# First layer's attention: inverse row sums reach the free axis by DMA through a row in memory, not by TensorE transposes and ScalarE copies

## The chip, the cores and the metric

The kernel runs on one core of a Trainium2 chip. The core has five engines with a queue of their own each: TensorE (PE, with its weight loads PEld), VectorE (DVE), ScalarE (ACT), GpSimd (POOL) and SyncE (SP), which here issues every DMA. Engines meet through semaphores only, and each works off its queue in order. The metric is device time in microseconds of one execution. Before the change it is 4202.77 us, the median of 3 runs (4202.66 to 4202.93).

## What is computed

The input is x of shape (8, 32, 32, 512) in float32. Two layers follow each other; the change touches the first alone, and of it this is what matters:

```python
x_flat = x.reshape(b, seq, c)                       # b = 8 images, seq = 1024 tokens, c = 512
x_norm = _group_norm(x, gn_scale, gn_bias).reshape(b, seq, c)
qkv = x_norm @ w_qkv + b_qkv
q, k, v = jnp.split(qkv, 3, axis=-1)                # then 8 heads of 64 channels
weight = jnp.einsum('bhld,bhsd->bhls', q * scale, k * scale)
weight = jax.nn.softmax(weight, axis=-1)
out = jnp.einsum('bhls,bhsd->bhld', weight, v)
out = out.transpose(0, 2, 1, 3).reshape(b, seq, c) @ w_out + b_out
return (x_flat + out).reshape(b, h, w, c)
```

The second layer (a layer norm, a deformable sampling, a second attention with 256 keys, an MLP) is the same in both kernels.

## The kernel before

`layer0` goes through the 8 images one after the other and through the 8 heads of an image in turn. For each engine a function writes out its whole queue for an image: `sync_image`, `tensor_image`, `scalar_image`, `vector_image`, `gpsimd_image`. The order of the work is therefore fixed by hand; nothing schedules it.

**Steps.** An image has U = 64 steps, 8 for a head, numbered `i_`. Step i computes the scores of 128 queries against all 1024 keys on TensorE (L446 and L447: high and low part of the keys, four products of 128x512). VectorE takes the row maxima (L624), ScalarE the exponentials with the row sums (L589). Two steps later TensorE transposes these probabilities (L461, eight 128x128 pieces), ScalarE copies them to SBUF as the high part `ph` (L582), VectorE makes the low part `pl` (L641).

**Blocks.** Two steps make a block b of 256 queries (32 blocks in an image, NB = 4 in a head). TensorE multiplies `ph` and `pl` of a block with the values in two halves, at steps 2b + 5 and 2b + 6 (L482, eight products of 128x256 each). High and low part of v stand side by side, so the result has two halves of 64 partitions which must be added: ScalarE copies one half (`fold_t`, L568), VectorE adds the other (`fold_s`, L632). At the end GpSimd multiplies by the inverse row sums and writes the block's attention into `qk` (L723).

**The inverse row sums.** VectorE makes them after every second step, at step 2b + 3 (L645), as `row_inv`, with a query on each partition. The multiplication needs a query in each column, the same value on all 64 partitions. Two TensorE transposes of the broadcast column (L477, at the head of the first half of the block's products) and a copy by ScalarE (`fold_r`, L572) bring them there. `fold_r` and `fold_s` have two buffers each.

**Staging of a head.** The scores of head H need its queries and keys split in high and low parts, doubled over the partitions. SyncE first brings them with four DMAs of 256 KB (L388, L389), once the scores of the first 8(H - 1) steps are done (L385), that is when head H - 1 is about to begin. GpSimd then splits them (`stage`): part 0 (L702, L704) after the multiplication of block 4H - 6, part 1 (L708, L711) after that of block 4H - 5, part 2 (L714) after that of block 4H - 4. This holds for heads 2 to 7, so six times in an image; heads 0 and 1 are staged ahead. TensorE's first score of head H waits for the end of part 2. A "head start" below is the start of that first product on L446.

**Queue of SyncE** in an image: the copies of heads 0 to 7; the next image's x (`xtok`, L394), once all copies have landed; x again for the residual (`tok`, L401); the stores of the result (L404).

## Time and profile before

| what | value |
|---|---|
| median of 3 runs | 4202.77 us |
| the profiled execution's own time | 4202.9 us |
| its span, first to last instruction | 4200.2 us |
| mean granted TensorE clock | 0.99 |
| attention of the first layer | 8 images, in the first 2320 us or so |
| busy share PE / DVE / ACT / POOL | 96% / 71% / 61% / 31% |
| TensorE instructions | 22762 |

The page's slices of the span show TensorE at nine tenths or more in nearly all of the first layer. Times in the rows further down are microseconds from the first instruction; "idle before" is how long an engine stood still before the piece of work, with what ended it. Matmuls overlap in the array, so the duration of one is not what it adds to the queue: the distance between two starts is.

### The profile page before, as it was taken

How to read it: one execution, taken by the hardware profiler on the slowest of the kernel's cores; microseconds unless marked ns; L12 is line 12 of the kernel's file. 1: busy time of each engine (PE TensorE's matmuls, PEld its weight loads, DVE VectorE, ACT ScalarE, POOL GpSimd, SP SyncE). 2: the span in 40 equal slices, each digit the busy share in tenths (PEclk: the TensorE clock that was granted, in tenths of full speed). 3: DMA queues.
4: the chain of work that ended last, by engine and by line, in shares of the span. 5: the costliest groups of instructions: out<-in, count | busy, mean ns of one | idle time of the engine just before them, and what ended most of it. 6: DMA issues, size and time to landing. Idle time of an engine off the chain costs nothing. (4 is left out here: it accounts for less than half of the span.)

```text
span 4200.2 us, 64531 instructions
## 1 busy us (share of the span) xinstructions
PE 4046.5 (96%) x22762; PEld 3386.1 (81%) x22762; DVE 2986.1 (71%) x5141; ACT 2582.9 (61%) x5617; POOL 1304.7 (31%) x1423
## 2 busy tenths in 40 slices
PE   8999999999999999999999899999999999999999
PEld 6888888888878888888888568777777777777777
DVE  3984975947849849669488367768696868686866
ACT  3874856837838658568387147564656565555646
POOL 1432433433324324324234004141323323141504
PEclk9999999999999999999999899999999999999999
DMA  2121220221212212212211303030302121212212
GB/s 83 41 69 43 49 83 21 61 61 39 58 46 51 67 44 63 61 31 51 61 41 50 115 21 86 18 99 21 92 29 71 51 61 61 61 61 53 69 39 62
DMA packets 113127, 235.53 MB, mean 56 GB/s; under 512 B 17260, under 2 KB 33704, under 8 KB 112808
## 3 DMA queue, kind: packets, MB, share of 16 engines
q1 hardware_dynamic: 112808, 231.41, 20.7%
q8 instruction: 184, 3.01, 0.3%
q14 instruction: 135, 1.11, 0.1%
HBM read 80.35 MB, written 33.55 MB: 27 GB/s over the span
## 5 line engine op out<-in xcount | busy, mean ns | idle before, releaser
L624 DVE TENSOR_REDUCE a_neg_max<-a_ps 128x1 f32<-128x1024 f32 x512 | 624.7, 1222 | 336.9 <-PE a_ps L447 336.9
L582 ACT ACTIVATE a_ph<-a_ps 128x512 fp32r<-128x512 f32 x1024 | 557.0, 593 | 171.2 <-PE a_ps L461 168.2
L641 DVE TENSOR_TENSOR a_pl<-a_ps,a_ph 128x512 fp32r<-128x512 f32 x1024 | 654.3, 679 | 8.9 <-ACT a_ph L582 5.7
L589 ACT ACTIVATE a_prob<-a_ps,a_neg_max 128x1024 f32<-128x1024 f32 x512 | 572.2, 1118 | 17.5 <-DVE a_neg_max L624 11.8
L723 POOL TENSOR_TENSOR a_qk<-a_fold_s,a_fold_r 64x256 f32<-64x256 f32 x256 | 191.3, 747 | 1228.4 <-DVE a_fold_s L632 1228.4
L461 PEld LDWEIGHTS a_ps<-a_ident,a_prob 128*128 128x128 f32 x4096 | 469.8, 140 | 112.6 <-issue 46.9
L461 PE MATMUL a_ps<-a_ident,a_prob 128*128 128x128 f32 x4096 | 540.7, 274 | 17.2 <-DVE a_pl L641 16.1
L1744 POOL TENSOR_SCALAR b_prob<-b_prob,b_row_inv 128x256 f32<-128x256 f32 x512 | 247.5, 483 | 994.4 <-DVE b_row_inv L1653 958.5
L482 PE MATMUL a_ps<-a_ph,a_v 128*128 128x256 f32 x2048 | 550.7, 302 | 0.0
L482 PE MATMUL a_ps<-a_pl,a_v 128*128 128x256 f32 x2048 | 509.1, 282 | 0.0
L446 PE MATMUL a_ps<-a_kh,a_qs 128*128 128x512 f32 x1024 | 408.3, 399 | 11.9 <-POOL a_kl L714 11.9
L447 PE MATMUL a_ps<-a_kl,a_qs 128*128 128x512 f32 x1024 | 404.7, 395 | 0.0
L482 PEld LDWEIGHTS a_ps<-a_pl,a_v 128*128 128x128 f32 x2048 | 389.3, 190 | 0.3
L482 PEld LDWEIGHTS a_ps<-a_ph,a_v 128*128 128x128 f32 x2048 | 386.4, 189 | 0.3
L1584 DVE SCALAR_TENSOR_TENSOR b_acc<-b_qpad,b_dww,b_acc 128x256 f32<-128x256 f32 x880 | 363.8, 479 | 4.9
L1250 PE MATMUL b_ps<-b_qpad,b_diag 128*128 128x256 f32 x1312 | 324.1, 408 | 0.0
L1429 ACT ACTIVATE b_diag<-b_ident,b_dww 128x128 f32<-128x128 f32 x656 | 250.6, 399 | 109.1 <-PE b_ps L1250 59.7
L1250 PEld LDWEIGHTS b_ps<-b_qpad,b_diag 128*128 128x128 f32 x1312 | 249.4, 190 | 72.8
L1506 ACT ACTIVATE b_prob<-b_ps,b_neg_max 128x256 f32<-128x256 f32 x512 | 236.4, 483 | 27.0 <-DVE b_neg_max L1658 26.6
L446 PEld LDWEIGHTS a_ps<-a_kh,a_qs 128*128 128x128 f32 x1024 | 193.7, 189 | 43.9 <-POOL a_kl L714 21.7
L447 PEld LDWEIGHTS a_ps<-a_kl,a_qs 128*128 128x128 f32 x1024 | 194.1, 190 | 25.0
L248 PE MATMUL a_ps<-a_xh,wqkv_hi 128*128 128x512 f32 x512 | 200.3, 391 | 4.3 <-DVE wqkv_lo L353 4.3
(250 smaller groups left out, 9058.4 us busy)
## 6 DMA issues: line engine op xcount, KB each, us to landing
a_qs<-a_qk SPq DMA_DIRECT2D x128, 256.0 KB, 3.7
a_kl<-a_qk SPq DMA_DIRECT2D x128, 256.0 KB, 4.4
a_xtok<-in_x SPq DMA_DIRECT2D x64, 256.0 KB, 4.4
b_xs<-x SPq DMA_DIRECT2D x64, 256.0 KB, 4.7
b_qs<-b_qh SPq DMA_DIRECT2D x64, 256.0 KB, 3.0
b_qs<-b_ql SPq DMA_DIRECT2D x64, 256.0 KB, 3.7
b_z<-x SPq DMA_DIRECT2D x64, 256.0 KB, 3.3
out<-b_ot SPq DMA_DIRECT2D x64, 256.0 KB, 2.0
```

Source lines behind the costliest of these rows:

```text
L446: pe.matmul(bank, q_, kh[:, j, n], start=True, stop=False)
L447: mm = pe.matmul(bank, q_, kl[:, j, n], start=False, stop=True)
L461: mm = pe.transpose(ps[:, 4 + n % 2, kk * P:(kk + 1) * P], prob[:, u % 2, kt * P:(kt + 1) * P], ident[:])
L482: mm = pe.matmul(ps[:, 6 + b % 2, 0:256], v[:, h, kt, :], q_[:, b % 2, kt, :], start=kt == 0 and e == 0, stop=kt == TT - 1 and e == 1)
L582: act.activation(ph[:, b % 2, 4 * g:4 * g + 4, (u % 2) * P:(u % 2 + 1) * P], ps[:, 4 + n % 2, :].rearrange("p (k q) -> p k q", k=4), ACT.C ...
L589: act.activation(prob[:, i_ % 2, :], ps[:, 2 * (i_ % 2):2 * (i_ % 2) + 2, :] .rearrange("p a b -> p (a b)"), ACT.Exp, bias=neg_max[:, i_:i ...
L624: dve.tensor_reduce(neg_max[:, i_:i_ + 1], ps[:, 2 * (i_ % 2):2 * (i_ % 2) + 2, :] .rearrange("p a b -> p (a b)"), AX, ALU.max, negate=Tru ...
L641: dve.tensor_tensor(pl[here], ps[:, 4 + n % 2, :].rearrange("p (k q) -> p k q", k=4), raw(ph[here]), ALU.subtract).then_inc(pl_ok, 1)
L1250: mm = pe.matmul(ps[:, c, 0:NS], diag[:, e % DIAGS, :], src, start=first, stop=last)
L1429: act.activation(diag[:, e % DIAGS, :], ident[:], ACT.Copy, scale=dww[:, c, n:n + 1])\
L1584: dve.scalar_tensor_tensor(dst, src, dww[:, c, n:n + 1], dst, ALU.mult, ALU.add)\
L1744: pool.tensor_scalar(prob[:, u % 2, t, :], prob[:, u % 2, t, :], row_inv[:, c:c + 1], 0.0, ALU.mult, ALU.add).then_inc(sc_ok, 1)
```

## The change

The two transposes (L477) and the copy into `fold_r` (L572) are gone. SyncE does the work instead: for each block, once `inv_ok` says that the inverses are there, it stores the two columns of `row_inv` (128 partitions, 8 bytes each) as a row of 256 values in memory, waits until this has landed, and loads that row back, broadcast to the 64 partitions that need it. The row then has the two steps' values alternating, so the multiplication reads `fold_r` with a step of two. `fold_cp` counts one copy in place of two, TensorE no longer waits for `inv_ok` and `fold_cp` in front of a block, and GpSimd waits for the load.

SyncE works in order, so these pairs of DMAs stand among the others. The copies of head H, which used to wait for nothing but the scores, now stand behind the pairs of blocks 0 to 4H - 5. The loads of the next image's x stand one behind each of the last eight pairs.

```diff
+            def inverses(b):
+
+                h = b // NB
+                sp.wait_ge(inv_ok, at(inv_ok, b + 1))
+                sp.dma_start(inv_row[b].rearrange("(p n) -> p n", n=2), row_inv[:, 2 * b:2 * b + 2]).then_inc(iv_st, 16)
+                sp.wait_ge(iv_st, at(iv_st, 16 * (b + 1)))
+                if b >= 2:
+                    sp.wait_ge(att_ok, at(att_ok, b - 1))
+                sp.dma_start(fold_r[own_half(h), b % 2, :], inv_row[b].partition_broadcast(HD))\
+                  .then_inc(iv_ld[b % 2], 16)
+
+            copies(0)
+            copies(1)
+            for b in range(U // 2):
+                if b % NB == 0 and b // NB + 1 in range(2, NH):
+                    copies(b // NB + 1)
+                if b == U // 2 - TT:
+                    for j in range(2):
+                        sp.wait_ge(s_ld[j], at(s_ld[j], 64 * (NH // 2)))
+                inverses(b)
+                if more and b >= U // 2 - TT:
+                    t = b - (U // 2 - TT)
                     sp.dma_start(xtok[:, t, :], x[r + 1, t * P:(t + 1) * P, :]).then_inc(x_ld[t], 16)
...
                 if part == 0:
-                    pe.wait_ge(inv_ok, at(inv_ok, b + 1))
...
-                        pe.wait_ge(fold_cp, at(fold_cp, 2 * b - 2))
-                    for n in range(2):
-                        u = 2 * b + n
-                        pe.transpose(ps[:, 6 + b % 2, 256 + n * P:256 + (n + 1) * P],
-                                     row_inv[:, u:u + 1].to_broadcast([P, P]), ident[:])
...
-                        .then_inc(fold_cp, 1)
-                    if b >= 2:
-                        act.wait_ge(att_ok, at(att_ok, b - 1))
-                    act.activation(fold_r[own_half(h), b % 2, :], ps[own_half(h), 6 + b % 2, 256:512], ACT.Copy)\
                         .then_inc(fold_cp, 1)
...
                 pool.wait_ge(fold_add, at(fold_add, b + 1))
-                pool.wait_ge(fold_cp, at(fold_cp, 2 * b + 2))
...
+                pool.wait_ge(iv_ld[b % 2], at(iv_ld[b % 2], 16 * (b // 2 + 1)))
...
+                                   fold_r[own_half(h), b % 2, :].rearrange("p (q n) -> p n q", n=2),
```

`copies(h)` holds the lines that stood in the loop over heads before, unchanged.

SyncE's queue from the start of an image, before: the copies of heads 0, 1, 2 and 3, four DMAs each.

```order
10 L388 DMA a_qs<-a_qk 64x1024 [waits a_qk_sb]
11 L389 DMA a_kl<-a_qk 64x1024
...
18 L388 DMA a_qs<-a_qk 64x1024 [waits a_score,a_qk_sb]
19 L389 DMA a_kl<-a_qk 64x1024
20 L388 DMA a_qs<-a_qk 64x1024
21 L389 DMA a_kl<-a_qk 64x1024
22 L388 DMA a_qs<-a_qk 64x1024 [waits a_score,a_qk_sb]
23 L389 DMA a_kl<-a_qk 64x1024
```

The same place after: `a_inv_row` is the row in memory; rows 24 and 25 are the pair of block 3, rows 26 to 29 the copies of head 2.

```order
22 L400 DMA a_inv_row<-a_row_inv 128x2 [waits a_inv_ok]
23 L404 DMA a_fold_r<-a_inv_row 64x256 [waits a_att_ok,a_iv_st]
24 L400 DMA a_inv_row<-a_row_inv 128x2 [waits a_inv_ok]
25 L404 DMA a_fold_r<-a_inv_row 64x256 [waits a_att_ok,a_iv_st]
26 L393 DMA a_qs<-a_qk 64x1024 [waits a_score,a_qk_sb]
27 L394 DMA a_kl<-a_qk 64x1024
28 L393 DMA a_qs<-a_qk 64x1024
29 L394 DMA a_kl<-a_qk 64x1024
30 L400 DMA a_inv_row<-a_row_inv 128x2 [waits a_inv_ok]
31 L404 DMA a_fold_r<-a_inv_row 64x256 [waits a_att_ok,a_iv_st]
```

What moved: the copies of a head have come to stand behind four pairs, each with a wait for a result of VectorE and a wait for its own store.

TensorE's queue at the first block's products, before (transposes of the probabilities, the two transposes of the inverses, the products):

```order
317 L461 MATMUL a_ps<-a_ident,a_prob 128x128 x8
318 L477 MATMUL a_ps<-a_ident,a_row_inv 128x128 x2
319 L482 MATMUL a_ps<-a_ph,a_v 128x256
320 L482 MATMUL a_ps<-a_pl,a_v 128x256
321 L482 MATMUL a_ps<-a_ph,a_v 128x256
```

And after, at the same place:

```order
317 L485 MATMUL a_ps<-a_ident,a_prob 128x128 x8
318 L500 MATMUL a_ps<-a_ph,a_v 128x256
319 L500 MATMUL a_ps<-a_pl,a_v 128x256
320 L500 MATMUL a_ps<-a_ph,a_v 128x256
```

What moved: nothing but the two transposes, which are gone; all else on TensorE keeps its order.

## Rows read from the trace of the kernel before

**Rows 1.** Groups by line: name, shapes, count | busy us, mean ns | idle before.

```profile
L477 PE MATMUL a_ps<-a_ident,a_row_inv 128*128 128x128 f32 x512 | 97.8, 273 | 0.6 <-DVE a_row_inv L645 0.6
```

**Rows 2.** Timeline of TensorE, two steps inside a head: start, us, line, work.

```profile
701.08 0.40 PE L446 MATMUL a_ps<-a_kh,a_qs 128*128 128x512 f32 x1
...
702.88 0.38 PE L477 MATMUL a_ps<-a_ident,a_row_inv 128*128 128x128 f32 x2
...
704.05 0.40 PE L446 MATMUL a_ps<-a_kh,a_qs 128*128 128x512 f32 x1
...
706.80 0.40 PE L446 MATMUL a_ps<-a_kh,a_qs 128*128 128x512 f32 x1
```

**Rows 3.** The same view around the starts of heads 1, 2, 3 and 7, third image.

```profile
689.62 0.40 PE L446 MATMUL a_ps<-a_kh,a_qs 128*128 128x512 f32 x1
...
712.41 0.28 PE L482 MATMUL a_ps<-a_pl,a_v 128*128 128x256 f32 x1
713.01 0.50 PE L446 MATMUL a_ps<-a_kh,a_qs 128*128 128x512 f32 x1 [0.32 <-POOL a_kl L714]
...
736.37 0.50 PE L446 MATMUL a_ps<-a_kh,a_qs 128*128 128x512 f32 x1 [0.18 <-POOL a_kl L714]
...
831.67 0.50 PE L446 MATMUL a_ps<-a_kh,a_qs 128*128 128x512 f32 x1 [0.18 <-POOL a_kl L714]
```

**Rows 4.** Timeline of SyncE and TensorE: the copies of head 3 after the last score.

```profile
710.47 0.39 PE L447 MATMUL a_ps<-a_kl,a_qs 128*128 128x512 f32 x1
...
710.94 0.46 SPq L388 DMA_DIRECT2D a_qs<-a_qk  x1
...
712.74 1.19 SPq L389 DMA_DIRECT2D a_kl<-a_qk  x1
```

**Rows 5.** DMA issues on L389: least, median and longest time to landing.

```profile
DMA to landing us min/median/max: 3.6/4.4/6.0
```

**Rows 6.** The same of the stores to memory on L404 (256 KB each).

```profile
DMA to landing us min/median/max: 2.0/2.0/4.1
```

**Rows 7.** Timeline of VectorE after the start of head 2.

```profile
714.24 1.23 DVE L624 TENSOR_REDUCE a_neg_max<-a_ps 128x1 f32<-128x1024 f32 x1 [0.85 <-PE a_ps L447]
715.50 0.43 DVE L632 TENSOR_TENSOR a_fold_s<-a_ps,a_fold_t 64x256 f32<-64x256 f32 x1
715.96 1.29 DVE L641 TENSOR_TENSOR a_pl<-a_ps,a_ph 128x512 fp32r<-128x512 f32 x2
717.22 1.22 DVE L624 TENSOR_REDUCE a_neg_max<-a_ps 128x1 f32<-128x1024 f32 x1
718.36 1.28 DVE L641 TENSOR_TENSOR a_pl<-a_ps,a_ph 128x512 fp32r<-128x512 f32 x2
719.55 0.15 DVE L645 RECIPROCAL a_row_inv<-a_row_sum 128x2 f32<-128x2 f32 x1
719.97 1.23 DVE L624 TENSOR_REDUCE a_neg_max<-a_ps 128x1 f32<-128x1024 f32 x1 [0.26 <-PE a_ps L447]
```

**Rows 8.** Timeline of GpSimd: end of head 2's staging, then the staging of head 3.

```profile
710.57 2.38 POOL L714 TENSOR_TENSOR a_kl<-a_kl,a_kh 128x1024 fp32r<-128x1024 f32 x1
...
722.62 1.05 POOL L702 TENSOR_SCALAR a_kh<-a_qs 128x1024 fp32r<-128x1024 f32 x1
723.75 2.40 POOL L704 TENSOR_TENSOR a_qs<-a_qs,a_kh 64x1024 fp32r<-64x1024 f32 x1
727.52 0.74 POOL L723 TENSOR_TENSOR a_qk<-a_fold_s,a_fold_r 64x256 f32<-64x256 f32 x1 [1.37 <-DVE a_fold_s L632]
...
733.11 0.74 POOL L723 TENSOR_TENSOR a_qk<-a_fold_s,a_fold_r 64x256 f32<-64x256 f32 x1 [2.60 <-DVE a_fold_s L632]
733.93 2.38 POOL L714 TENSOR_TENSOR a_kl<-a_kl,a_kh 128x1024 fp32r<-128x1024 f32 x1
```

**Rows 9.** Who waited for L714: engine and line, us in total, times.

```profile
  PE a_ps L446: 11.9, 48
```

**Rows 10.** Timeline of TensorE: first scores of images 4, 5 and 6, and a wait.

```profile
1238.89 0.39 PE L446 MATMUL a_ps<-a_kh,a_qs 128*128 128x512 f32 x1
...
1525.22 0.39 PE L446 MATMUL a_ps<-a_kh,a_qs 128*128 128x512 f32 x1
...
1748.87 0.73 PE L508 MATMUL a_ps<-wout_hi,a_a 128*128 128x512 f32 x1 [2.19 <-DVE a_tok_a L656]
...
1813.18 0.39 PE L446 MATMUL a_ps<-a_kh,a_qs 128*128 128x512 f32 x1
```

**Rows 11.** Stretches: length, busy us by engine, granted clock (PEclk), DMA share, GB/s.

```profile
15.10:25.10 10.00, 4.62 (x6) 2.07 (x7) 8.58 (x16) 6.55 (x6) 1.02 (x1) 0.50 0.42 161
...
1749.00:1752.40 3.40, 3.40 (x9) 2.63 (x10) 3.40 (x5) 1.43 (x2) 0.00 (x0) 0.50 0.28 108
886.00:892.00 6.00, 3.77 (x17) 2.82 (x16) 6.00 (x7) 3.18 (x3) 1.53 (x1) 1.00 0.12 44
```

**Rows 12.** Timeline of ScalarE at the last block of an image.

```profile
867.96 0.38 ACT L572 ACTIVATE a_fold_r<-a_ps 64x256 f32<-64x256 f32 x1
```

More of the change, by code:

```diff
@@ L84, in layer0 @@
     QSCALE = 1.0 / HD
+    inv_row = nc.dram_tensor("a_inv_row", [U // 2, 256], F32, kind="Internal").ap()
     with ExitStack() as ctx:
@@ L161, in layer0 @@
         av_ps, fold_cp, fold_add, att_ok = sem("av_ps"), sem("fold_cp"), sem("fold_add"), sem("att_ok")
+        iv_st, iv_ld = sem("iv_st"), [sem(f"iv_ld{i}") for i in range(2)]
         ah_ok, al_ok, out_ps, res_ok, out_ok = sem("ah_ok"), sem("al_ok"), sem("out_ps"), sem("res_ok"), sem("out_ok")
@@ L164, in layer0 @@
                    xn_ok, xh_ok, xl_ok, pr_ps, qk_sb, vh_ok, vl_ok, staged, score, max_ok, exp_ok, tr_ps, ph_ok,
-                   pl_ok, inv_ok, av_ps, fold_cp, fold_add, att_ok, ah_ok, al_ok, out_ps, res_ok, out_ok]
+                   pl_ok, inv_ok, av_ps, fold_cp, fold_add, att_ok, iv_st, *iv_ld, ah_ok, al_ok, out_ps, res_ok, out_ok]
         nums = [s.num for s in cleared]
@@ L366, in layer0 @@
         EACH.update({s_ld[0].num: 256, s_ld[1].num: 256, o_st.num: 16 * TT, pr_ps.num: len(groups), qk_sb.num: n_qk})
-        EACH.update({s.num: U for s in (score, max_ok, exp_ok, fold_cp)})
+        EACH.update({s.num: U for s in (score, max_ok, exp_ok)})
         EACH.update({s.num: 2 * U for s in (tr_ps, ph_ok, pl_ok)})
-        EACH.update({s.num: U // 2 for s in (inv_ok, av_ps, fold_add, att_ok)})
+        EACH.update({s.num: U // 2 for s in (inv_ok, av_ps, fold_cp, fold_add, att_ok)})
+        EACH.update({iv_st.num: 16 * (U // 2), iv_ld[0].num: 16 * (U // 4), iv_ld[1].num: 16 * (U // 4)})
         EACH.update({staged.num: STAGE * NH, ah_ok.num: len(SPLIT_AT), al_ok.num: len(SPLIT_AT)})
@@ L379, in sync_image, with copies @@
             more = r + 1 < n_images
-            for h in range(NH):
+            def copies(h):
                 p, j = h // 2, h % 2
@@ L389, in sync_image @@
                     sp.dma_start(raw(kl[rows_, j, :]), qk[own_half(h), CT + p, :]).then_inc(s_ld[j], 16)
-            if more:
-                for j in range(2):
-                    sp.wait_ge(s_ld[j], at(s_ld[j], 64 * (NH // 2)))
-                for t in range(TT):
+            def inverses(b):
[18 more added lines that the diff above has]
+                    t = b - (U // 2 - TT)
                     sp.dma_start(xtok[:, t, :], x[r + 1, t * P:(t + 1) * P, :]).then_inc(x_ld[t], 16)
@@ L494, in out_tile @@
                     pe.wait_ge(fold_add, at(fold_add, U // 2 + t - 3))
-                    pe.wait_ge(fold_cp, at(fold_cp, U + 2 * (t - 3)))
                 else:
@@ L628, in vector_image @@
                     h = b // NB
-                    dve.wait_ge(fold_cp, at(fold_cp, 2 * b + 2))
+                    dve.wait_ge(fold_cp, at(fold_cp, b + 1))
                     if b >= 2:
@@ L721, in gpsimd_image @@
                 pool.wait_ge(fold_add, at(fold_add, b + 1))
-                pool.wait_ge(fold_cp, at(fold_cp, 2 * b + 2))
-                pool.tensor_tensor(qk[own_half(h), h // 2, (b % NB) * 256:(b % NB + 1) * 256],
-                                   fold_s[own_half(h), b % 2, :], fold_r[own_half(h), b % 2, :],
+                pool.wait_ge(iv_ld[b % 2], at(iv_ld[b % 2], 16 * (b // 2 + 1)))
+                pool.tensor_tensor(qk[own_half(h), h // 2, (b % NB) * 256:(b % NB + 1) * 256]
+                                   .rearrange("p (n q) -> p n q", n=2),
+                                   fold_s[own_half(h), b % 2, :].rearrange("p (n q) -> p n q", n=2),
+                                   fold_r[own_half(h), b % 2, :].rearrange("p (q n) -> p n q", n=2),
                                    ALU.mult).then_inc(att_ok, 1)
```

## The prediction

> **What bounds the kernel now.** I read the groups by line first, then the timelines of one head. TensorE is busy for 96% of the span. Two steps inside a head show what that means [rows 2]: the first scores start at 701.08, 704.05 and 706.80. The interval that holds the two transposes of the inverses is 2.97 us, the one without is 2.75 us, and TensorE stands still in neither. So it is TensorE's queue that sets the pace inside a head. The second thing to see is at a head's start [rows 3]. The last product of head 1 starts at 712.41, the products before it are 0.12 apart, so head 2 could start at 712.53; it starts at 713.01, released by GpSimd's L714. In all 48 staged heads TensorE waits for that line [rows 9]. The wait is small, but it says that GpSimd's staging ends just as it is needed: **whatever makes the staging later makes the head later, one for one.** From head 1 to head 7 of an image it is 831.67 - 689.62 = 142.05 us, so 23.68 us for each of six heads. Of this, 0.48 is the wait and 4 x 0.22 = 0.88 the transposes; TensorE by itself would need about 22.1 to 22.3 us after the change.
>
> **What is removed.** The profile's groups by line put 97.8 us on the transposes [rows 1], but matmuls overlap; the distance of starts gives 2.97 - 2.75 = 0.22 us for a pair. Times 256 blocks that is 56 us, if TensorE stays the bound. ScalarE loses a copy of 0.38 us in each block. It has slack inside a head, and the copy lies on the path only at the last block of an image, where it stands between TensorE's last product and the attention's end [rows 12].
>
> **What is added, and where it stands.** A store of 128 x 8 bytes, a wait for its landing, a load of 64 x 1 KB, for each of 256 blocks. For the multiplication itself these are hidden: the inverses of a block are ready at step 2b + 3, its sum is folded at step 2b + 6, some 7 us later, and a store and a load come to about 2 + 2 us by the stores' landing [rows 6]. VectorE just keeps up: two steps are 719.55 + 0.15 - 714.24 = 5.46 us of work for it, with one fold and one reciprocal in them [rows 7], against 2 x 2.75 = 5.50 us of TensorE. The loads of the next image and of the residual come later by some microseconds, and lie behind other work of TensorE at an image's end.
>
> **What is moved is the point.** The copies of head H leave SyncE's queue behind the pair of block 4H - 5. Before, they leave 0.08 us after the last score of head H - 2 has ended, so ahead of the start of head H - 1 (710.47 + 0.39 = 710.86, first copy 710.94) [rows 4]. Now they wait for the reciprocal of step 8H - 7, which falls behind the start of head H - 1, then for a store. That makes a closed loop from one head start to the next:
>
> 1. Head start to the end of the reciprocal: 719.55 + 0.15 - 713.01 = 6.69 us [rows 3, 7]. VectorE is busy without a gap from 714.24 on, so TensorE's missing transposes don't shorten this.
> 2. Hand over to SyncE: 0.08 [rows 4].
> 3. The store to its landing: not in the trace. Nearest are the 256 KB stores to memory, 2.0 at least and in the median, 4.1 at most [rows 6]. The new one moves 1 KB, but in 128 pieces; I take 2.0, since the 256 KB stores are the only stores there are, and keep 4.1 as the other end. Below 2.0 nothing in these rows goes.
> 4. Hand over 0.08, and the load's issue 0.5, as one copy's (0.46 us, the next right behind) [rows 4].
> 5. The four copies: the last is issued 712.74 - 710.94 = 1.80 after the first and lands 4.4 (median of both places) to 6.0 later [rows 4, 5]; as the last of four it waits behind the others, so I take 5.2, the middle: 7.0.
> 6. Hand over 0.08.
> 7. GpSimd's chain from part 0 to the end of part 2, with the multiplications of blocks 4H - 5 and 4H - 4 between, which are ready by then: 733.93 + 2.38 - 722.62 = 13.69 as it stands, less the two waits of 1.37 and 2.60, plus 0.08 for each of two gaps: 9.88 [rows 8]. The multiplication now reads `fold_r` with a step of two; no row has that. Bounds are 0 and the operation's own 0.74 us, twice, and nothing below 0, as it works on as many values as before. I take 0, since 64x256 in 0.74 us is the pace of one value after the other in any case.
> 8. GpSimd's end to TensorE's first product: 713.01 - 712.95 = 0.06 (L714 of head 2 ends 710.57 + 2.38 = 712.95) [rows 3, 8].
>
> Sum: 6.69 + 0.08 + 2.0 + 0.58 + 7.0 + 0.08 + 9.88 + 0.06 = **26.37 us**, against 23.68 before and some 22.2 that TensorE needs. So TensorE stands still for about 4 us at each of the 48 starts, and the gain inside the heads is swallowed: what TensorE saves, it waits longer.
>
> **The clock.** TensorE's waits in the first layer so far are 2.2 us at most [rows 10]. After such a wait of 2.19 us in image 5 the granted clock was 0.50 for 3.4 us, the 1.2 GHz level, while after the like wait of image 2 it stayed at 1.00, the 2.4 GHz level; at the kernel's start, with waits of 4 us and more, it was 0.50 for 10 us [rows 11]. The half-clock stretch cost image 5 (1813.18 - 1525.22) - (1525.22 - 1238.89) = 1.63 us. Waits of 4 us at each head should bring it about most times. In the loop TensorE has a part only in term 1, through two steps' scores, so I price it at half of that cost, 0.8 us for a head, with bounds 0 and 1.6.
>
> The Trainium skill, "TensorE: Matmul & The Clock Gate", section "Why this matters for your kernels", asks to avoid gaps of some microseconds between bursts of matmuls, since the clock goes back to half after them. By the Trainium skill each head start here would come at the half clock; by the 2.2 us waits of this trace, one of which brought the half level and one of which did not, it could be none. The difference between the two is the 38 us of this term.
>
> **Sum.** (26.37 + 0.8 - 23.68) x 48 = 167.5 us. The first of the six loops in an image starts at a head that did not wait, 0.2 us less, x 8 = -1.6. Outside the six loops an image keeps about seven pairs of transposes, 7 x 0.22, and the last copy, 0.38: 1.9 x 8 = -15.2. Span 4200.2 + 150.7 = 4350.9; the execution's time is 2.7 us over its span (4202.9, which is the median within 0.2), so **4354 us**, 3.6% slower.
>
> **Rivals.**
> - *The clock holds* (no half level at head starts): 38 us less, 4316. For it speaks the 2.2 us wait of image 2, which left the clock alone; against it that 4 us is nearly twice that, and the start of the kernel. Chance 0.22.
> - *Small pieces are dear*: the store takes up to 4.1 us, or the strided multiplication up to 1.5 us more in the loop, or the four copies 6.0 instead of 5.2. Each microsecond in the loop is 48 us. With one of them at its end and the others where I have them: 4392 to 4455. Chance 0.18. The Trainium skill, "DMA: Bandwidth & Descriptors", section "Specifications", says that pieces under 512 bytes are done by read-modify-write, which would speak for a store over 2.0 us; no row of this trace has such a store.
> - *The staging keeps its cover*, and TensorE's 0.22 us a block is the gain: 4202.9 - 56 = 4147, and a bit less if the 0.5 us waits of the heads go too. The point at which it decides is a loop under 22.2 us: 4.2 us would have to be missing from my 26.37. That needs copies that land in 2.8 us instead of 7.0, or a queue of SyncE in which they don't wait for the store. The queue is plain to read, and every large term is a row. Chance 0.05.
> - *No difference*: the loop comes out near 23.4 us, 3 us under the sum, by copies that land faster and a quick store. Chance 0.02.
>
> **How the numbers follow.** Forecast 0.50 for 4330 to 4390, clock holds 0.22, dear pieces 0.18, cover 0.05, no difference 0.02, and 0.03 for a wait at the images' ends that I took as hidden. The likeliest gives 4354. The low end of the range takes in the steady clock with copies a bit under 7.0: 4285. The high end takes one dear piece nearly whole, 4450. Left out are the cases of no loss and both dear pieces together, less than 2 in 10. Faster 0.05, same 0.02, slower 0.93; 0.2% is about what a measurement of this kernel can tell from no change.
>
> **What would show it.** In the profile after, the distance of head starts should be about 27 us, with a wait of 3.5 to 4.5 us before L470 (the scores' first line there) released by GpSimd, 48 times, 170 to 200 us in total. GpSimd's first staging line (L702 before) should wait for the copies' DMA at heads 2 to 7, which it does at heads 0 alone now. Steps inside a head should be 2.75 us all. The new store's landing shows term 3, the multiplication's mean term 7, the granted clock in the first steps of a head the clock term. If the waits stand at another place, or the steps are not 2.75, the reading is wrong.

## The result, and the profile after

The kernel after takes 4533.62 us (median of 4 runs, 4527.79 to 4536.18) against 4202.72 us before in the same rounds: a ratio of 1.079, 95% interval 1.077 to 1.081. The forecast was 4354 with a range of 4285 to 4450. **The direction and the mechanism came as forecast, the size did not: the loss is 331 us, not 151.** The profiled execution took 4535.13 us with a span of 4533.4.

What the waits of the kernel after say (from the list of waits: who waited <- for whom: us in total, times, the longest):

```profile
POOL a_kh L715 <- DMA a_kl<-a_qk: 620.1, 56, 36.4
...
PE a_ps L470 <- POOL a_kl L727: 266.4, 48, 8.7
...
POOL a_qk L736 <- DMA a_fold_r<-a_inv_row: 182.2, 31, 44.6
```

L470 is the scores' first line (L446 before), L715 and L727 the first and last line of the staging (L702 and L714 before). Where 48 head starts waited 11.9 us in total [rows 9], they now wait 266.4; and GpSimd's staging now waits for the copies at 56 heads, all but the 8 heads 1. Both are the places that the prediction named. The last of these lines is one that it did not name: in 31 places a multiplication waits for its row. Of these, 22 are the last three blocks of an image, 29 to 31; in blocks 4 to 28, where the loops are, it is 7. The 44.6 us are an image's first block, which waited as long before (44.8 at most, for VectorE's fold).

One head start and the steps behind it on TensorE, third image (start, us, work; answers to [rows 2, 3]):

```profile
828.86 0.79 PE L470 MATMUL a_ps<-a_kh,a_qs 128*128 128x512 f32 x1 [5.52 <-POOL a_kl L727]
...
833.67 0.40 PE L470 MATMUL a_ps<-a_kh,a_qs 128*128 128x512 f32 x1
...
836.41 0.40 PE L470 MATMUL a_ps<-a_kh,a_qs 128*128 128x512 f32 x1
...
839.17 0.40 PE L470 MATMUL a_ps<-a_kh,a_qs 128*128 128x512 f32 x1
...
840.86 1.16 PE L485 MATMUL a_ps<-a_ident,a_prob 128*128 128x128 f32 x8 [0.60 <-DVE a_pl L654]
...
842.81 0.40 PE L470 MATMUL a_ps<-a_kh,a_qs 128*128 128x512 f32 x1
...
858.56 0.80 PE L470 MATMUL a_ps<-a_kh,a_qs 128*128 128x512 f32 x1 [4.45 <-POOL a_kl L727]
```

The steps that begin at 833.67 and 836.41 take 2.75 us, and the 2.97 of the steps with transposes is gone: their gain is there. But it is not whole. The step that begins at 839.17 takes 3.64 us, since TensorE waits 0.60 us for VectorE's `pl` in it. Heads 3, 5 and 7 have such a step (3.37 us before), heads 2, 4 and 6 have two of 2.88. The first step takes 4.81 us, and from this head's start to the next it is 29.70 us, where it was 23.68 on average before. The stretch behind the start (length, busy us of PE, PEld, DVE, ACT and POOL with counts, granted clock, DMA share, GB/s):

```profile
829.00:835.00 6.00, 6.00 (x28) 5.29 (x29) 3.07 (x5) 2.29 (x4) 0.73 (x1) 0.66 0.06 14
```

The same 6 us behind a head start before, right behind the one at 713.01 [rows 3]:

```profile
713.00:719.00 6.00, 5.99 (x43) 5.55 (x44) 5.09 (x9) 4.80 (x11) 0.74 (x1) 1.00 0.69 143
```

TensorE is busy all the time in both, but does 28 pieces of work in place of 43: granted clock 0.66, a mixture of the 1.2 and the 2.4 GHz level. By the trace's granted clock all 48 staged heads start at the half level. The half-clock stretch begins 0.5 to 5.1 us before the start, so inside the wait, and goes on for 2.9 to 6.1 us behind it, 4.8 in the mean. The page's slices, each some four heads long, show it only faintly, six of the first 25 at 8 tenths (one before):

```profile
PEclk9999899899999899899999898999999999999999
```

The other members of the loop in the same head. VectorE (answers to [rows 7]; the bracket is the idle time before):

```profile
830.97 1.23 DVE L637 TENSOR_REDUCE a_neg_max<-a_ps 128x1 f32<-128x1024 f32 x1 [5.17 <-PE a_ps L471]
...
834.79 1.23 DVE L637 TENSOR_REDUCE a_neg_max<-a_ps 128x1 f32<-128x1024 f32 x1 [0.80 <-PE a_ps L471]
...
837.13 0.15 DVE L658 RECIPROCAL a_row_inv<-a_row_sum 128x2 f32<-128x2 f32 x1
```

SyncE (answers to [rows 4]): the pair of the block, the four copies, the next pair.

```profile
837.31 0.33 SPq L400 DMA_DIRECT2D a_inv_row<-a_row_inv  x1
840.14 0.44 SPq L404 DMA_DIRECT2D a_fold_r<-a_inv_row  x1
840.68 0.54 SPq L393 DMA_DIRECT2D a_qs<-a_qk  x1
...
842.56 1.21 SPq L394 DMA_DIRECT2D a_kl<-a_qk  x1
...
849.92 0.46 SPq L404 DMA_DIRECT2D a_fold_r<-a_inv_row  x1
```

GpSimd (answers to [rows 8]):

```profile
848.66 1.06 POOL L715 TENSOR_SCALAR a_kh<-a_qs 128x1024 fp32r<-128x1024 f32 x1 [7.68 <-DMA a_kl<-a_qk]
...
852.28 0.73 POOL L736 TENSOR_TENSOR a_qk<-a_fold_s,a_fold_r 64x256 f32<-64x256 f32 x1
...
856.16 2.34 POOL L727 TENSOR_TENSOR a_kl<-a_kl,a_kh 128x1024 fp32r<-128x1024 f32 x1
```

Read as a chain: 828.86 start; 837.28 reciprocal done (8.42); 837.31 store leaves, 840.14 it has landed (2.83); 840.68 first copy, 848.66 the staging can begin (7.98); 858.50 it ends (9.84); 858.56 next head. Nothing in it is idle by choice, each link waits for the one before.

Landing times of the store (L400), then of the load (L404), least, median and longest of 256:

```profile
DMA to landing us min/median/max: 2.6/4.2/7.4
...
DMA to landing us min/median/max: 2.5/3.5/7.1
```

At the end of an image TensorE now waits where it did not (third image, the longest of seven, TensorE's first transpose of the next image's x; the others wait 1.9 to 4.2 us; before, this wait was 0.81 us):

```profile
995.17 1.09 PE L191 MATMUL a_ps<-a_ident,a_xtok 128*128 128x128 f32 x4 [5.01 <-ACT a_xt L195]
```

and GpSimd's last multiplication, one of the 31:

```profile
993.36 0.73 POOL L736 TENSOR_TENSOR a_qk<-a_fold_s,a_fold_r 64x256 f32<-64x256 f32 x1 [7.24 <-DMA a_fold_r<-a_inv_row]
```

### The profile page after: what moved, and what is told of

It reads as the page before. It is cut to its first block and busy times, and to the rows that moved or that the text cites. A ratio compares the mean times of both kernels' runs of the same rounds, so it can differ in the third digit from the quotient of the medians.

```text
span 4533.4 us, 63988 instructions
## 1 busy us (share of the span) xinstructions
PE 4111.8 (91%) x22250; PEld 3430.7 (76%) x22250; DVE 2994.5 (66%) x5141; ACT 2508.0 (55%) x5361; POOL 1306.1 (29%) x1423
## 5 line engine op out<-in xcount | busy, mean ns | idle before, releaser
L470 PE MATMUL a_ps<-a_kh,a_qs 128*128 128x512 f32 x1024 | 435.8, 426 | 266.4 <-POOL a_kl L727 266.4
L485 PE MATMUL a_ps<-a_ident,a_prob 128*128 128x128 f32 x4096 | 588.5, 289 | 21.7 <-DVE a_pl L654 20.6
L485 PEld LDWEIGHTS a_ps<-a_ident,a_prob 128*128 128x128 f32 x4096 | 502.4, 148 | 134.9 <-issue 72.3
L500 PE MATMUL a_ps<-a_ph,a_v 128*128 128x256 f32 x2048 | 576.9, 312 | 0.0
L500 PE MATMUL a_ps<-a_pl,a_v 128*128 128x256 f32 x2048 | 530.5, 290 | 0.0
L470 PEld LDWEIGHTS a_ps<-a_kh,a_qs 128*128 128x128 f32 x1024 | 208.4, 204 | 301.0 <-POOL a_kl L727 276.1
L471 PE MATMUL a_ps<-a_kl,a_qs 128*128 128x512 f32 x1024 | 427.5, 417 | 0.0
L500 PEld LDWEIGHTS a_ps<-a_pl,a_v 128*128 128x128 f32 x2048 | 409.0, 200 | 0.3
L500 PEld LDWEIGHTS a_ps<-a_ph,a_v 128*128 128x128 f32 x2048 | 408.0, 199 | 0.5 <-issue 0.2
L715 POOL TENSOR_SCALAR a_kh<-a_qs 128x1024 fp32r<-128x1024 f32 x64 | 67.4, 1053 | 620.8 <-DMA a_kl<-a_qk 620.1
L471 PEld LDWEIGHTS a_ps<-a_kl,a_qs 128*128 128x128 f32 x1024 | 209.5, 205 | 27.4
```

The source lines that it names most:

```text
L470: pe.matmul(bank, q_, kh[:, j, n], start=True, stop=False)
L471: mm = pe.matmul(bank, q_, kl[:, j, n], start=False, stop=True)
L485: mm = pe.transpose(ps[:, 4 + n % 2, kk * P:(kk + 1) * P], prob[:, u % 2, kt * P:(kt + 1) * P], ident[:])
L500: mm = pe.matmul(ps[:, 6 + b % 2, 0:256], v[:, h, kt, :], q_[:, b % 2, kt, :], start=kt == 0 and e == 0, stop=kt == TT - 1 and e == 1)
```

## The experiments

The theory is the prediction's closed loop: reciprocal, store, copies, staging, next head. Rivals are the clock, the small pieces and contention as the larger part. "Loop" below is the mean distance from one head start to the next over the 40 that end at heads 3 to 7 of the 8 images, where the loop is settled. The ratios are to the kernel before, timed beside each (4202.33, 4204.71, 4204.67 and 4202.63 us in the four groups of runs).

**e1_hoist: the copies ahead of the pairs again.**

```diff
-                if b % NB == 0 and b // NB + 1 in range(2, NH):
-                    copies(b // NB + 1)
+                if b % NB == 2 and b // NB + 2 in range(2, NH):
+                    copies(b // NB + 2)
```

> The changed kernel with one thing moved in SyncE's queue: the four copies of head H stand ahead of the pair of block 4H - 6, not behind the pair of block 4H - 5, so they leave when the scores of head H - 2 are done, as in the kernel before. Theory (the loss is the closed loop reciprocal, store, copies, staging): TensorE's waits at the 48 head starts fall from 266 us in total to under 20 us, a head takes about 22.3 us, and the time is 4202.9 - 56 plus the some 4 us by which each image's end got longer (gap before the transposes of the next image, 5.0 against 0.8 us), x 8: about 4180 us. Rival (the pairs of DMAs are themselves what costs: small pieces land after 4.2 us, the rows come after 3.5 us, and GpSimd's multiplications wait for them wherever the copies stand): heads stay above 26 us and the time above 4350.

Measured: 4337.44 us, ratio 1.033 (1.031 to 1.035), 196 us less than after. So the place of the copies is the larger part of the loss, but the 4180 us of the theory were missed by 157: the settled heads are 25.7 to 26.3 us apart, not 22.3. The rest is a new wait in the other direction: the row of block 4H - 6 now stands behind copies that wait for a score, and comes late. The multiplications of blocks 2, 6, 10, 14, 18 and 22 wait 6.4 to 11.4 us for it. The list of waits:

```profile
POOL a_qk L736 <- DMA a_fold_r<-a_inv_row: 764.9, 160, 44.6
...
PE a_ps L470 <- POOL a_kl L727: 119.8, 48, 5.9
```

The rival, that the pairs cost this wherever the copies stand, is answered by e10_inter below: the same pairs in memory, with heads of 23.1 to 24.0 us.

**e2_late: the kernel before with nothing but late copies.** The transposes stay, there are no pairs; the copies of a head wait for four scores more.

```diff
-                    sp.wait_ge(score, at(score, TT * (h - 1)))
+                    sp.wait_ge(score, at(score, TT * (h - 1) + 4))
```

> The kernel before, with its transposes and ScalarE copies, no pair of DMAs, and one thing changed: SyncE holds the copies of head H back until four more score steps are done (so until some 10 us after the start of head H - 1 at the full clock, 12 at the half one, where the changed kernel sends them at 12.2). Theory of the closed loop: the lateness alone makes the loss. Loop 12 + 7.0 + 0.1 + 9.9 = 29 us with the clock at half after the starts, 27 us if it holds, against 23.7: 4202.9 + 48 x 3.3 to 5.3 = 4360 to 4460 us, waits on GpSimd at 48 heads of 4 to 5 us each. Rival (traffic and latency of the new DMAs make the loss): hidden or nearly so, under 4250.

Measured: 4451.89 us, ratio 1.059 (1.058 to 1.061). Three quarters of the loss of the change, without one of its DMAs. TensorE's waits for the staging:

```profile
PE a_ps L446 <- POOL a_kl L714: 166.9, 48, 4.6
```

The first copy leaves 11.85 us behind the head start on average (12.30 in after), and the loop is 28.73 us. Lateness alone makes the loop; its clock came with it (mean 0.964, before 0.99).

**e3_busy: TensorE kept busy through the wait.** At each staged head start, 40 products of 128x256 whose result is overwritten come ahead of the wait for the staging, and behind the one for the exponentials; only work is added.

```diff
+                if t == 0:
+                    if h >= 2:
+                        for _ in range(40):
+                            pe.matmul(ps[:, 2 * (i_ % 2), 0:256], woh[:, 0, 0:P], woh[:, 1, 0:256], start=True,
+                                      stop=True)
+                    pe.wait_ge(staged, at(staged, STAGE * (h + 1)))
```

> The changed kernel with 40 products of 128x256 more on TensorE at each staged head's start, written to a bank that the head's first scores then overwrite, so that TensorE works where it stood still (some 4.8 us of work in a wait of 5.6). Theory (half clock after the wait costs 2.1 us of the loop, in the stretch from head start to the reciprocal: 8.8 us in place of 6.7): the granted clock stays at 1.0, that stretch is 6.7 us, the loop 28 us in place of 30.1, and the time falls by 48 x 2.1 = 100 us to about 4430, though TensorE has 230 us more to do. Rival (the clock is a symptom, the stretch is long for other reasons): the time stays at 4534 or rises.

Measured: 4463.83 us, ratio 1.0625 (1.061 to 1.064): 1920 useless products made the kernel 70 us faster. The stretch behind a head start (columns as above):

```profile
812.60:818.60 6.00, 6.00 (x42) 5.51 (x43) 4.79 (x7) 3.79 (x7) 0.75 (x1) 1.00 0.14 11
```

The granted clock is 1.00 in place of 0.66, 42 pieces in place of 28. From head start to the end of the reciprocal it is 6.75 us on average (after: 8.70), as expected. The loop is 28.92 (after: 30.55), so 1.63 us of the 1.95 arrive; the store and GpSimd's chain take 0.3 us longer here. That is the larger part of why 70 us came and not the 100 of the expectation.

**e4_wide: whole rows of 512 bytes in place of 8-byte pieces.** The store is made from `ident`, so values other than the inverses are loaded.

```diff
+    inv_row = nc.dram_tensor("a_inv_row", [U // 2, P * P], F32, kind="Internal").ap()
...
+                sp.dma_start(inv_row[b].rearrange("(p n) -> p n", n=P), ident[:]).then_inc(iv_st, 16)
...
+                sp.dma_start(fold_r[own_half(h), b % 2, :], inv_row[b, 0:256].partition_broadcast(HD))\
```

> The changed kernel with the store of each pair taken from the identity matrix, 128 pieces of 512 bytes in place of 128 pieces of 8; the row that is loaded back is part of that, so the attention is multiplied by other values than its inverse row sums. Theory (the store's 2.9 us when alone, where 256 KB stores take 2.0, is due to pieces of 8 bytes): it lands after 2.0 to 2.1 us, the loop is 0.8 us shorter, and the time falls by 40 us to about 4495. Rival (it is the price of a store next to the others, or of its 128 pieces whatever their size): within 10 us of 4534, or above it.

Measured: 4378.52 us, ratio 1.0415 (1.040 to 1.043): 155 us less than after, four times the 40 that I expected. Moving 64 times the bytes, the store lands sooner, and the load behind it too. L400, then L404:

```profile
DMA to landing us min/median/max: 1.5/1.5/5.1
...
DMA to landing us min/median/max: 2.4/2.5/3.5
```

This was the surprise, and the next kernels ask what about the pieces is slow.

**e7_pitch and e11_pitch64: the same 8-byte pieces, laid apart.** 512 bytes and 64 bytes from one to the next; the load reads 1 KB of mostly other values, and the rows in memory are filled once at the start.

```diff
+                sp.dma_start(inv_row[b].rearrange("(p n) -> p n", n=P)[:, 0:2], row_inv[:, 2 * b:2 * b + 2])
```

```diff
+                sp.dma_start(inv_row[b, 0:16 * P].rearrange("(p n) -> p n", n=16)[:, 0:2], row_inv[:, 2 * b:2 * b + 2])
```

> The changed kernel with the 128 pieces of 8 bytes stored 512 bytes apart in memory, each into a line of its own; the row that is loaded back is the first 1 KB there, so most of the attention is multiplied by other values than its inverses, and 32 stores at the start of the first image set the rest of the memory. Theory (a piece of 8 bytes is dear by itself): the store lands after 2.8 us or more as before. Rival (dear is that many pieces share a line of memory and are done one after the other): it lands after 1.5 to 1.6 us as the pieces of 512 bytes do, and the loop falls to 27.3 us.

> As e7_pitch, with the 8-byte pieces 64 bytes apart in place of 512, so eight of them in 512 bytes; most of the attention is multiplied by other values than its inverses. If the crowding is within 64 bytes, the store lands after 1.4 us as in e7_pitch; if within 512 bytes, between 1.4 and 2.9 us.

**e8_p256: pieces of 256 bytes side by side**, again from `ident`.

```diff
+                sp.dma_start(inv_row[b, 0:64 * P].rearrange("(p n) -> p n", n=64), ident[:, 0:64]).then_inc(iv_st, 16)
```

> As e4_wide, the store from the identity matrix and other values than the inverses, but with pieces of 256 bytes: two pieces share what one of 512 fills. If pieces under 512 bytes pay a read-modify-write each, it lands after 2.8 us as the 8-byte ones. If only the crowding of many pieces in a line costs, it lands at 1.5 to 1.8 us.

Measured: e7_pitch 4361.75 us, ratio 1.037 (1.035 to 1.039); e11_pitch64 4361.15, 1.037 (1.036 to 1.039); e8_p256 4364.57, 1.038 (1.036 to 1.040). All three agree with e4_wide within 18 us. The store of e11_pitch64 (L401), then of e8_p256 (L400):

```profile
DMA to landing us min/median/max: 1.4/1.4/4.7
```

```profile
DMA to landing us min/median/max: 1.4/1.4/4.8
```

So the number of pieces is not it, nor their size: 128 pieces of 8 bytes land in 1.4 us when each has 64 bytes to itself, and in 2.6 at the least when they are packed side by side. Pitches between 8 and 64 bytes were not run. The loads are 2.5 us in all three. Since these kernels load other memory than was written in small pieces, or only some of it, they don't tell whether the load of after is slower because its row was packed or because it was just then written; that stays open.

**e5_sbrow: the row in SBUF instead of in memory**, on one partition.

```diff
+        inv_row = R.take("a_inv_row", [1, 2, 256])
...
+                sp.dma_start(inv_row[:, b % 2, :].rearrange("o (p n) -> o p n", n=2), row_inv[:, 2 * b:2 * b + 2])
...
+                sp.dma_start(fold_r[own_half(h), b % 2, :], inv_row[:, b % 2, :].unsqueeze(1).to_broadcast([1, HD, 256]))\
```

> The changed kernel with the row of inverses kept in SBUF (one partition, two buffers) in place of memory: the same 128 pieces of 8 bytes, the same queue order, and the wait for the multiplication two blocks back ahead of the store. Theory (8-byte pieces are dear only when they are written to memory): the store lands after 2.0 us or less, the load after 2.0 to 2.5, the loop is 27.3 us as with the 512-byte pieces, and the time is 4350 to 4390 us. Rival (128 pieces of 8 bytes are dear wherever they go): the store lands after 2.8 us or more and the time stays at 4500 or above.

Measured: 4501.26 us, ratio 1.070 (1.068 to 1.072), 32 us less than after. Its store (L402), then its load (L404):

```profile
DMA to landing us min/median/max: 1.9/1.9/5.2
...
DMA to landing us min/median/max: 3.8/4.0/4.4
```

The theory missed by more than 110 us: its store came, its load did not. The time is the rival's, but not by the rival's slow store. In the loop the store gives 1.0 us (2.99 to 1.98), but the load lands later (4.0 for 3.5 us in the median), and the four copies behind it take 8.43 us from first issue to last landing (after: 7.94). **Here half of what the quicker store won went to slower copies behind a slower load.**

**e6_sbhoist, e9_sbinter and e10_inter: the copies moved back, with less in their way.** e6 is e5 with e1's edit. e9 is e5 with the copies between the store and the wait for it; e10 is the same with the row in memory.

```diff
+                if b % NB == 2 and b // NB + 2 in range(2, NH):
+                    copies(b // NB + 2)
                 sp.wait_ge(iv_st, at(iv_st, 16 * (b + 1)))
```

> e5_sbrow with the copies of head H two blocks earlier in SyncE's queue, as in e1_hoist. Theory (two causes and no third: copies behind the pairs, and slow pairs): both gone, the heads are bound by TensorE at 22.2 to 22.6 us, no half clock at their starts, and the time is 4150 to 4185 us, faster than the kernel before. Rival (SyncE's one queue is too busy in any case, store, wait, load and copies of 3 us in turn, so that GpSimd's multiplications still wait for a row): heads of 24 us or more, 4230 or above.

> The row of inverses in SBUF, and the copies of head H issued between the store and the load of block 4H - 6, so that SyncE issues them while that store is on its way (in e6_sbhoist they stood ahead of that store, the pair came 3 to 5 us late and the staging's first part waited for its multiplication). Theory: the multiplication of block 4H - 6 waits 1 to 2 us less for its row, the staging ends before the head is due, the waits at head starts fall under 0.2 us, a head takes 22.4 us in the mean, and the time is about 4130 us (4115 to 4150). Rival: the load now queues behind 1 MB of copies and lands no sooner, so heads stay at 23.4 us and the time at 4175 to 4190.

> The changed kernel, row in memory, with the copies of head H between the store and the load of block 4H - 6. Same theory: against e1_hoist (4337) the copies no longer hold back a pair, heads come down from 26.2 to 24 to 25 us, 4230 to 4290, still above the kernel before since store (4.2 to 4.7 us) and load (3.5 to 3.7 us) of every block fill SyncE's 5.5 us. Rival: if the slow stores were slow through the copies running beside them, heads at 22.5 us and 4150.

Measured: e6_sbhoist 4180.78 us, ratio 0.995 (0.993 to 0.996); e9_sbinter 4180.58, 0.994 (0.993 to 0.996); e10_inter 4206.77, 1.000 (0.9995 to 1.001). So one place in SyncE's queue turns a loss of 331 us into nothing (e10), and with the row in SBUF into a small gain. The expectations fared worse than that sounds. e6's time lies in its range, but its heads take 23.1 to 23.9 us and not 22.2 to 22.6, so the number was right by another way. e9 was expected at 4130 and came at its rival's 4175 to 4190: issuing the copies behind the store, not ahead of it, gave nothing over e6. e10 came below its 4230 to 4290. The settled heads of e9 and e10 are nearly alike inside an image (23.1 and 23.9 to 24.0 us by turns); what parts them is the image's end, 119 to 121 us from head 7 to the next image's first score in e9, 122 to 128 in e10. There the last multiplication waits for its row in all 8 images, 5.3 to 7.6 us, and the wait before L191 is 3.1 to 8.5 us (e9: under 0.8).

But 56 us were to be had from the transposes and 24 came. GpSimd before a head start of e9_sbinter shows one reason:

```profile
795.07 0.74 POOL L736 TENSOR_TENSOR a_qk<-a_fold_s,a_fold_r 64x256 f32<-64x256 f32 x1 [0.42 <-DMA a_fold_r<-a_inv_row]
...
797.02 1.05 POOL L724 TENSOR_SCALAR a_kh<-a_kl 128x1024 fp32r<-128x1024 f32 x1
800.25 0.76 POOL L736 TENSOR_TENSOR a_qk<-a_fold_s,a_fold_r 64x256 f32<-64x256 f32 x1 [2.17 <-DVE a_fold_s L645]
801.09 2.37 POOL L727 TENSOR_TENSOR a_kl<-a_kl,a_kh 128x1024 fp32r<-128x1024 f32 x1
```

Part 2 of the staging (L727) stands behind the multiplication of block 4H - 4, which waits 2.17 us for VectorE's fold. TensorE's next head starts at 803.51, right behind it. The staging hangs on a fold late in the head.

**e12_sbparts and e13_bparts: part 2 right behind part 1**, ahead of that multiplication; e12 on e9, e13 on the kernel before.

```diff
-                if 1 <= k <= NH - 2 and part < 3:
-                    stage(k + 1, (part,))
+                if 1 <= k <= NH - 2 and part < 2:
+                    stage(k + 1, ((0,), (1, 2))[part])
```

> e9_sbinter with part 2 of a head's staging moved from behind the multiplication of block 4H - 4 to behind part 1, so behind block 4H - 5. In e9_sbinter and e10_inter heads take 23.07 and 23.89 us in turn, though TensorE needs some 22.1, and L727 ends just before each start. Theory: what is left of the removed transposes' gain is eaten by that one wait, since part 2 hangs on the fold of step 8H - 2 and not on TensorE's queue. Then heads fall to 22.1 and 23.0 us, waits at the 48 starts vanish, and the time falls by 48 x 0.9 = 43 us to about 4138. Rival (VectorE, with 5.46 us of work for each 5.50 us, is the floor): heads come down by 0.3 us or less, 4165 to 4180.

> The kernel before, transposes and all, with only that move of part 2. By the theory above its heads lose only the waits of 0.5 and 0.2 us at their starts, 48 x 0.35 = 17 us, to about 4186, and the difference to e12_sbparts (48 us expected) is what taking the transposes off TensorE is worth once nothing else binds; 56 us was my figure for it. Rival (VectorE is the floor): both end at the same time.

Measured: **e12_sbparts 4155.27 us, ratio 0.989 (0.987 to 0.990), the fastest of all, below both kernels**; I had put it at 4138. e13_bparts 4197.20, 0.9985 (0.998 to 0.999), expected at 4186. In its heads the expected 17 us came (the six loops of an image fell from 142.05 to 139.96 us). But six of its seven image ends hold a half-clock stretch of 3.4 us, which the kernel before has in one, and they take 122.6 us in the mean for 121.1. GpSimd of e12:

```profile
786.72 1.05 POOL L724 TENSOR_SCALAR a_kh<-a_kl 128x1024 fp32r<-128x1024 f32 x1
787.85 2.40 POOL L727 TENSOR_TENSOR a_kl<-a_kl,a_kh 128x1024 fp32r<-128x1024 f32 x1
790.32 0.74 POOL L736 TENSOR_TENSOR a_qk<-a_fold_s,a_fold_r 64x256 f32<-64x256 f32 x1
```

L727 ends at 790.25, the next head starts at 792.94, and in the list of waits no row of TensorE behind L727 is left. The difference of e13 and e12 is 4197.20 - 4155.27 = 42 us, where 56 was the forecast of what the transposes are worth. It is not all theirs. By the spans (43.7 us) the six loops make 23 of it, the way from head 0 to head 1 makes 3, and the images' ends 18; some 6 of these are the half-clock stretch, which e12 has at two images' ends and e13 at six. Inside the six loops 42 us were forecast (24 pairs, 8 images, 0.22 us), so about half of it came. The other half did not come: some steps take 2.88 us for 2.75, with waits too short for the list, and some 3.6, where TensorE waits for the next in line, VectorE. List of waits of e12_sbparts (16.1 us in 48 places before, 25.0 in 72 in e13):

```profile
PE a_ps L485 <- DVE a_pl L654: 33.4, 72, 0.6
```

VectorE has 5.46 us of work in two steps, TensorE now 5.50. In heads 3, 5 and 7 VectorE has an operation more, twice: a low part of the attention (L662), with a wait for ScalarE in front of it. In the head of after shown above it stands ahead of TensorE's wait at 840.86:

```profile
837.97 0.69 DVE L662 TENSOR_TENSOR a_a<-a_qk,a_a 128x512 fp32r<-128x512 f32 x1 [0.68 <-ACT a_a L610]
```

In e12 TensorE waits 0.5 to 0.6 us for `pl` behind each of the two, these steps take 3.64 and 3.58 us, and the settled heads come 22.4 and 23.9 us apart by turns. The rival of e12, VectorE as the floor, had the time wrong but this part of the mechanism right.

**e14_xearly: the next image's x loaded ahead of the last eight pairs**, all eight at once, to see whether the wait at the image's end is for them.

```diff
+                    if more:
+                        for t in range(TT):
+                            sp.dma_start(xtok[:, t, :], x[r + 1, t * P:(t + 1) * P, :]).then_inc(x_ld[t], 16)
```

> The changed kernel with the eight loads of the next image's x issued together ahead of the pair of block 24, as in the kernel before, and not one behind each of the last eight pairs. Theory A (each image's end is 4 us longer because the last block's row comes late, behind those loads in the queues): the wait before the transposes of x at an image's end falls from 5.0 to about 1 us, and the time falls by 25 to 30 us to some 4505. Theory B (the row is late by its own slow store and load): the wait stays at 4 to 5 us and the time within 10 us of 4534, or rises as block 24 now waits behind 2 MB.

Measured: 4582.08 us, ratio 1.090 (1.088 to 1.092), 48 us slower than after. In the third image the wait before L191 went from 5.0 to 2.2 us, in the mean of seven images from 3.2 to 1.9, so the loads are a part of it. The larger part is the slow store and load, theory B: in e4_wide and e11_pitch64, where the loads of x stand as in after, that wait is gone and no last multiplication waits for its row. But the 2 MB went in front of block 24's pair; part 2 of head 7's staging stands behind that block's multiplication, and the loop into head 7 grew to 36.5 to 38.2 us in the seven images that have such loads. An image's end won little, 123.7 us in the mean (122.3 to 124.5) against 124.8.

## Where the prediction held, and which steps failed

The terms of the loop, from the trace of each kernel, each a mean of its 40 settled loops:

| term, us | forecast | after | e3_busy | e4_wide | e11_pitch64 | e5_sbrow |
|---|---|---|---|---|---|---|
| 1, 2: start to reciprocal, handover, clock | 7.57 | 8.73 | 6.78 | 8.08 | 8.09 | 8.84 |
| 3: store to landing | 2.0 | 2.99 | 3.17 | 1.53 | 1.52 | 1.98 |
| 4: handover, load's issue | 0.58 | 0.58 | 0.58 | 0.58 | 0.56 | 0.62 |
| 5: four copies | 7.0 | 7.94 | 7.97 | 7.09 | 7.02 | 8.43 |
| 6, 7, 8: handovers, GpSimd's chain | 10.02 | 10.31 | 10.44 | 10.08 | 10.10 | 10.27 |
| loop | 27.17 | 30.55 | 28.92 | 27.35 | 27.30 | 30.14 |

- **The mechanism held.** The copies behind a pair close a loop from head start to head start; 48 waits before L470, all released by GpSimd. e2_late makes such a loop without the pairs, e6, e9 and e10 undo it, e1 in part. The rival that the staging keeps its cover (deciding point: a loop under 22.2 us) was not near.
- **The steps held in part.** Most take 2.75 us inside a head, and the distance from head 0 to head 1 fell from 23.39 to 22.96 us, as two pairs of transposes there make it. But "2.75 us all" and "TensorE's queue sets the pace" were read from head 1 and the even heads 2 to 6. In heads 3, 5 and 7 one step took 3.37 us before, with TensorE waiting for VectorE, and takes 3.64 now. What removing the transposes is worth in the loops is therefore about half of 0.22 us a pair (e12 against e13). That e12 and e13 differ by 42 us, near the 56, is partly luck, by the images' ends.
- **Term 3 was mis-sized, 2.0 for 2.99.** "Below 2.0 nothing in these rows goes" was right of the rows and wrong of the chip: e11_pitch64's store took 1.4. I took 2.0 because the only stores in the trace had it; the row could not say what 8-byte pieces packed side by side do. The rival with dear pieces was this one, at 4.1 us for the store; in the loop it was half way there, over all blocks in the median at 4.2, and it did not come alone.
- **Term 5 was mis-sized, 7.0 for 7.94.** The pair in front of the copies was given its issue time (term 4) but no effect on them. Where its load landed in 2.5 us (e4, e11) the copies took 7.0 to 7.1, in after with 3.5 it was 7.9, with e5's 4.0 it was 8.4; without any pair (e2) 6.8. It is not the next pair, behind the copies: that store is issued 4.15 us behind the first copy, and by then the first copy is already 0.9 us late (it lands 4.18 us behind its issue, 3.27 in e11). That the load itself does it is argued: it is what is on its way at that time, but from loop to loop in after its landing and the copies' do not go together.
- **With quick pieces the loop is 27.30 us, against my 27.17, and that is luck.** In e11 the store is 0.48 us under my term and the clock's stretch 0.52 over it; the two errors cancel. The e11 time of 4361 us, near my 4354, says nothing for the sum either.
- **The clock was mis-sized, 0.8 for about 2.0.** e3_busy shows it (8.70 to 6.75 for term 1). I took half of 1.63, the cost of a half-clock stretch of 3.4 us [rows 11], on the ground that TensorE has a part only through two steps' scores. The halving was the wrong step. Between the first scores and the second stands TensorE's whole step, transposes and products too: 4.81 us here where 2.75 is the full-clock step, and the second scores, at 833.67, already run at full speed. In e4_wide, where 3.4 us at half clock lie behind most starts, term 1 is 8.06 us, and 6.48 in the one head without any: 1.6 us, the whole price of rows 11. In after it is 4.8 us at half clock in place of 3.4, so the upper bound of 1.6 was too low as well.
- **Term 7 held.** The multiplication with a step of two is 0.74 us in the median, as before, so zero was right. The chain is 0.22 us over the 9.88. That the rows are hidden from the multiplications held inside the loops and failed in blocks 29 to 31.
- **The image's end was wrong in sign.** I took 1.9 us an image off and called waits there hidden; from head 7 to the next image's first score it is 124.8 us for 121.1 before, where I had 119.2. The row of the last block lands late, so the last multiplication waits 7.24 us in the third image (5.6 to 7.2 in all), and head 7 starts at half clock too. "Lie behind other work" had no row behind it. Without the late row (e11) it is 121.7 us, and with a full clock at head 7 as well (e9) 120.0: some 3 us are the late row with its own half-clock stretch, some 2 the clock behind head 7.

The miss, by span: 4533.4 - 4350.9 = 182.5 us. Of it the 48 loops are 8 x 180.96 - (27.17 x 48 - 1.6) = 145 us, the rest of the images 37 (about +22 measured for -15.2 forecast). The first loop of an image is 28.21 us, not 0.2 but 2.3 under the others, as the head that opens it has no wait and no half clock. By the table the settled loop's excess of 3.4 us is 1.2 clock, 1.0 store, 0.9 copies and 0.3 the handovers and GpSimd. The three larger ones were all on the same side, and I had a case for one at a time. That is the fault of the range: packed pieces raised terms 3 and 5 together, and the longer wait came with more half-clock time (waits of 3.0 us and 3.4 us at half clock in e4, 5.5 and 4.8 in after, in the mean).

The rule of the Trainium skill, "TensorE: Matmul & The Clock Gate", section "Why this matters for your kernels", that such gaps bring the clock back to half, holds for the waits of 4.0 to 8.7 us here: all 48 staged heads start at the half level. In e3_busy, which fills most of each wait, 43 of 48 heads have no half-clock time behind their start. The Trainium skill, "DMA: Bandwidth & Descriptors", section "Specifications", says that pieces under 512 bytes are done by read-modify-write. Whether they are, no run here shows. By size alone it had no price in the landing time: pieces of 256 bytes landed in 1.4 us, those of 512 bytes in 1.5, and of 8-byte pieces only the packed ones were slow.

**Open:** which part of the path makes packed pieces slow (8 bytes apart they are, 64 bytes apart they are not, more is not shown); whether the load is slower for the packing or for the fresh write; by what the copies behind it are held up.

## What to carry to other kernels

In an engine's in-order queue, a step that waits for a result pulls everything behind it into its wait: before moving a DMA into a queue, list what is behind it and when that used to leave. Here the pairs cost 331 us in front of the copies. With the copies issued between a store and its load the same pairs cost nothing (4206.77 against 4204.67), and with the row in SBUF as well 24 us were gained. And when a chain has closed on itself, price it with the dear cases together: here the store, the copies behind the pair and the clock were all dear at once.

## What the runs showed of the hardware

- A store of 128 pieces of 8 bytes packed side by side in memory took 2.6 us at the least and 4.2 in the median. Laid 64 or 512 bytes apart, or as pieces of 256 bytes, it took 1.4. The load behind it took 3.5 in the first case and 2.5 in the others.
- Behind waits of 4.0 to 8.7 us TensorE started at half clock each time and stayed there for another 2.9 to 6.1 us. 40 products without use in each wait gave 70 us back.
- A half-clock stretch of 3.4 us cost 1.6 us of TensorE's time, at head starts of e4_wide as at an image's end before.
- One partition of SBUF read 64 times by a load of 64 KB landed in 4.0 us, 1.5 us more than the like load from memory in e4_wide. Into SBUF the packed 8-byte pieces landed in 1.9.
- An operand read with a step of two on GpSimd cost nothing that shows: 0.744 us in the median, with unit steps 0.737.
